# Fewer waits for landed gathers on GpSimd, merge's copies in four parts, and another order of SyncE's waits

## The reference, cut to what matters

```python
# block 0: Gaussian-mixture convolution, K = 3
gauss = exp(sum(-0.5 * (attr - mu)**2 / (1e-14 + sigma**2)))      # per edge, 3 weights
msg   = einsum('eko,ek->eo', (x[src] @ g).reshape(E, 3, 64), gauss)
aggr  = segment_sum(msg, dst) / max(count(dst), 1)
y     = silu(aggr + x @ root_w + bias + x)
# block 1: two SAGE layers on the same edges
nbr   = segment_sum(h[src], dst) / max(count(dst), 1)
h     = h @ W_self + nbr @ W_neigh + b                            # relu between the two
```

## Time and profile before

| | |
|---|---|
| median of 3 runs | 7992.47 us |
| the profiled execution's own time | 8047.77 us |
| its span | 8045.9 us |
| busy: TensorE, VectorE, ScalarE, GpSimd | 64%, 54%, 34%, 42% of the span |
| L512, GpSimd's gathers | 3136 of 1071 ns mean, 3357.8 us busy, 2680.9 us idle before them |
| the long stage, by GpSimd's gathers | from about 61 us to about 6040 us |

### The profile page before, as it was taken

The page is one execution under the profiler, slowest core; times in us unless marked ns, Lnnn a source line. Parts: engine busy times, 40 slices in busy tenths (PEclk is TensorE's granted clock), DMA queues, the critical chain, the costliest instruction groups (busy, mean ns, idle before and its releaser), DMA issues.

```text
span 8045.9 us, 144868 instructions
## 1 busy us (share of the span) xinstructions
PE 5141.5 (64%) x35195; PEld 4042.1 (50%) x35196; DVE 4379.7 (54%) x15088; ACT 2772.2 (34%) x8317; POOL 3360.0 (42%) x3146
## 2 busy tenths in 40 slices
PE   1555555555555555555555555555554699999999
PEld 1223333333444444443334333443443699999999
DVE  5667778766777666655555555555553422222222
ACT  3112333334444444455555555555451100000000
POOL 5013444445666666666666666666650000000000
PEclk5557888877787787777777777777775699999999
DMA  2001111112222222222222222222221399999998
GB/s 68 28 23 56 55 65 65 64 64 68 85 85 85 85 70 86 85 79 75 85 85 76 78 85 85 73 80 85 85 84 42 134 381 382 381 368 385 385 384 346
DMA packets 258352, 1082.32 MB, mean 135 GB/s; under 512 B 140102, under 2 KB 144230, under 8 KB 194406
## 3 DMA queue, kind: packets, MB, share of 16 engines
q1 hardware_dynamic: 142806, 968.66, 31.2%
q0 software_dynamic: 100352, 102.96, 5.6%
q10 hardware_dynamic: 14902, 8.11, 0.5%
HBM read 751.67 MB, written 327.81 MB: 134 GB/s over the span
## 4 chain that ended last, share of the span: by engine, by line
PE 34%; issue 19%; DVE 18%; DVEq 12%; POOL 7%; DMA 4%; ACT 3%; another core or an unknown queue 1%; SPq 1%; ACTq 0%; POOLq 0%
PE pw L965 20%; POOL rE L512 7%; PE pw L795 6%; DVE rE L1264 5%; PE pw L820 3%; DVEq L1297 3%; DVEq L1467 3%; DMA rE<-in_x,idx 2%; DVE rE L1262 2%; DVE rE L1324 2%; PE pw L767 2%; DVE rE L1390 1%; DMA tab<-tab_d 1%; DVE rE L1389 1%; DVEq L1264 1%
## 5 line engine op out<-in xcount | busy, mean ns | idle before, releaser
L512 POOL DMA_INDIRECT rE<-in_x,idx x3136 | 3357.8, 1071 | 2680.9 <-issue 2495.7
L795 PE MATMUL pw<-rE 128*128 128x193 f32 x7824 | 1774.0, 391 | 946.3 <-DVE rE L1324 813.8
L595 ACT CAST rB<-pw 128x792 bf16<-128x792 f32 x1568 | 1252.7, 813 | 3247.8 <-PE pw L820 1081.7
L795 PEld LDWEIGHTS pw<-rE 128*128 128x128 f32 x7824 | 1620.9, 232 | 1163.7 <-DVE rE L1324 983.0
L558 ACT ACTIVATE rE<-rE,cols 128x64 f32<-128x64 f32 x4704 | 1255.0, 344 | 9.3 <-DMA tab<-tab_d 8.2
L820 PE MATMUL pw<-rE 128*128 128x396 f16 x3840 | 822.3, 362 | 669.8 <-DVE rE L1264 471.2
L1264 DVE TENSOR_SCALAR rE<-iperm,gr 128x392 f16<-128x392 f16 x3840 | 1062.3, 317 | 9.7 <-issue 8.8
L820 PEld LDWEIGHTS pw<-rE 128*128 128x128 f16 x3840 | 370.4, 104 | 1060.1 <-DVE rE L1264 547.1
L814 PE MATMUL pw<-rE 128*128 128x396 f16 x1600 | 449.0, 396 | 648.2 <-DVE rE L1390 483.9
L965 PE MATMUL pw<-rB,rA 128*128 128x192 bf16 x9604 | 810.8, 246 | 0.1
L965 PE MATMUL pw<-rE,rA 128*128 128x192 bf16 x9604 | 810.4, 246 | 0.1
(11 more groups left out here) (256 smaller groups left out, 2669.2 us busy)
## 6 DMA issues: line engine op xcount, KB each, us to landing
rA<-count SPq DMA_DIRECT2D x392, 1568.0 KB, 8.4
count<-rB SPq DMA_DIRECT2D x98, 3136.0 KB
rE<-in_x,idx POOLq DMA_INDIRECT x3136
cols<-cols_d SPq DMA_DIRECT2D x98, 64.0 KB
cols_d<-rA SPq DMA_DIRECT2D x3, 1568.0 KB, 5.2
rA<-in_edge_attr ACTq DMA_DIRECT2D x1, 4608.0 KB
out<-gcol ACTq DMA_DIRECT2D x97, 32.0 KB, 6.0
count<-rB SPq DMA_DIRECT2D x8, 224.0 KB, 2.0
```

The lines of the kernel that those rows point to most:

```text
L512: pool.indirect_dma_start(out=gath[:, s, u * CB + b, :], out_offset=None, in_=x, in_offset=bass.IndirectOffsetOnAxis(ap=idx[:, s, u * CB + ...
L595: act.copy(stage[:, s, :, j * 2 * W:(j + 1) * 2 * W].rearrange("p h (w n) -> p w h n", w=2), pu[j % 3][:, :, 0:CW].rearrange("p w (h n) -> ...
L795: ins = pe.matmul(sums[side][:, 0:AW], onehot[:, side, bb, :], wgath[:, side, bb, :], start=(bb == 0), stop=(bb == CB - 1))
```

## The change

Four edits:

1. GpSimd waits for landed gathers (L516) only behind groups 1 and 3 of a tile. Behind groups 0 and 2 it goes on to the waits for the next group's place.
2. In SyncE's pass the wait for the four groups of tile t + 1 and the load of the indices of tile t + 3 move from the pass's start to its end.
3. `merge_ahead(t + 1)` moves from behind unit n = 9 to behind unit n = 4.
4. ScalarE's 32 copies, which stood behind unit 12, are made in four parts of 8, behind units 6, 7, 8 and 9. Only in tile 47, where the copies for tile 48 are made, they stay in one piece behind unit 12.

```diff
             def after(part, t, s, last=False, rows=True):
                 base = PARTS[part][0]
-                if rows:
-                    for u in range(U):
-                        sp.wait_ge(a_g[1 - s][u], (t + base + s) * (8 * CB) + 16 * CB)
-                        sp.sem_inc(s_tick[4], 1)
-                    load_idx(t + (base + 3), 1 - s)
                 sp.wait_ge(a_evac, t * NU + (base * NU + NU + 2))
 ...
                     load_cols(t + (base + 2), s)
+                if rows:
+                    for u in range(U):
+                        sp.wait_ge(a_g[1 - s][u], (t + base + s) * (8 * CB) + 16 * CB)
+                        sp.sem_inc(s_tick[4], 1)
+                    load_idx(t + (base + 3), 1 - s)
```

```diff
-                        pool.wait_ge(a_g[s][u], 16 * CB * (i + 1))
-                        pool.sem_inc(s_tick[1], 1)
+                        if u % 2:
+                            pool.wait_ge(a_g[s][u], 16 * CB * (i + 1))
+                            pool.sem_inc(s_tick[1], 1)
```

```diff
-            def copied(t, s):
-                act.wait_ge(a_mrg, t * 8 + (2 - 8 * TM))
-                act.sem_inc(s_tick[2], 1)
-                act.load(places, tab[0:1, s * TW_:s * TW_ + T_B0])
-                for j in range(JW):
+            def copied(t, s, part=None):
+                if not part:
+                    act.wait_ge(a_mrg, t * 8 + (2 - 8 * TM))
+                    act.sem_inc(s_tick[2], 1)
+                    act.load(places, tab[0:1, s * TW_:s * TW_ + T_B0])
+                for j in range(JW) if part is None else range(8 * part, 8 * part + 8):
...
-                ins.then_inc(a_mrg, 1)
+                if part is None or part == 3:
+                    ins.then_inc(a_mrg, 1)
...
-                        if merged and j == NU - 4:
+                        if merged == "first" and j == NU - 4:
                             copied(i * 2 + (s + 1), 1 - s)
+                        if merged == "parts" and 6 <= j < 10:
+                            copied(i * 2 + (s + 1), 1 - s, j - 6)
```

```diff
-                        if n == NU // 2 + 1 and not last:
+                        if n == 4 and not last:
                             merge_ahead(t + 1)
```

More of the change, by code:

```diff
@@ L573, in copied, with windows @@
                     ins = act.copy(both[:, :, j], gr[:, bass.ds(at, 2)])
-                ins.then_inc(a_mrg, 1)
-            def windows(i, s, last, merged=False):
+                if part is None or part == 3:
+                    ins.then_inc(a_mrg, 1)
+            def windows(i, s, last, merged=None):
                 act.wait_ge(a_st[s], 16 * i + 1)
@@ L611, in _ @@
             windows(TM // 2 - 1, 0, False)
-            windows(TM // 2 - 1, 1, False, True)
+            windows(TM // 2 - 1, 1, False, "first")
             with act.Fori(0, (NT - TM) // 2 - 1, 1) as i:
                 for s in range(2):
-                    windows(i + TM // 2, s, False, True)
-            windows(NT // 2 - 1, 0, False, True)
+                    windows(i + TM // 2, s, False, "parts")
+            windows(NT // 2 - 1, 0, False, "parts")
             windows(NT // 2 - 1, 1, True)
```

## The result

The changed kernel takes 7649.33 us (median of 4 runs, 7645.0 to 7651.4) where the kernel before takes 7993.4 (median of 4, 7985.57 to 8002.84). The ratio is 0.957, 95% interval 0.955 to 0.959: 344 us less. Forecast were 7732 and 260 us less; the time lies in the range, at its fast end. The profiled execution took 7651.4 us, its span is 7649.6.

What follows compares the result with a forecast made beforehand. GpSimd's gather row was taken to bound the kernel, 53.8 us a tile. GpSimd would give 79 + 204 = 283 us, the users 248; 260 was taken, 8048 to 7788 profiled, 7732 as median, range 7640 to 7880.

Steps and rivals of the forecast that it cites:

- GpSimd paces, and two landing waits of four go: GpSimd's gather row sets the tile; two gaps fall from 2.79 to 0.30 us, 5.0 us a tile, to 48.8.
- The price of store against landing: SyncE's store at random phases stretches GpSimd's landing waits by up to 5.7 us; 0.9 us a tile taken.
- R1: Store locks onto GpSimd's landing wait, or VectorE's `tab` wait counts fully: pace 51 to 52.5, 7837 to 7912 us; 22%.
- merge_ahead and the copies: VectorE waits 5 us more for `tab` at unit 4, 3.0 less for copies; users' pace 47.1 to 49.1.
- the stretch before tile 48: Users gain only 18 us over 25 tiles at 51.0; tile 48's gathers start at 3271, 79 us earlier.
- Tiles 0 to 23 stay: The first tiles gain nothing from the change; tiles 6 to 15 stay at 71 us a tile.
- The indices behind the store: Index loads leave later; GpSimd begins up to 7 us later, covered by 16.63 us idle: nothing, at most 7 once.
- The second rule: Denser VectorE doesn't lengthen GpSimd's gathers (1.056 against 1.057 us): nothing; if it did, 0.4 us a tile, 20 in all.
- R3: Faster still: stores miss the landing waits, VectorE's ring hides `tab`; pace 48.8 or less, 7662 us or below; 5%.
- R2: GpSimd's group boundary without landing wait isn't free, about half of 2.79 us stays: pace 51, 7837 us; 7%.
- R4: Sixteen gathers can't be under way, the ninth waits for the queue: GpSimd's tile stays, 7992 us; 3%.
- R5: Slower: full `tab` wait at unit 4 plus a landing wait stretched 5.7 us every tile; 8057 us at 55.5; 6%.

Runs made afterwards that it cites:

- e8_sp_alone: The kernel before with only SyncE's new order (wait for tile t + 1's gathers and index load moved to the pass's end): 8151.49 us, ratio 1.019.
- e13_pool16_behind_store: The kernel before with one landing wait in sixteen gathers, and a tile's first gather waiting for the last issued store to land: 7629.79 us, ratio 0.954.
- e4_pool_and_sp: The kernel before with one landing wait in sixteen gathers and SyncE's new order, merge_ahead and copies as before: 7618.65 us, ratio 0.953.
- e5_wait_once_in_32: The changed kernel with one landing wait in thirty-two gathers, at a tile's end: 7637.35 us, ratio 0.955 to the kernel before.
- e11_pool32_and_sp: The kernel before with SyncE's new order and one landing wait in thirty-two gathers, merge_ahead and copies as before: 7481.29 us, ratio 0.935.
- e7_pool16_tiny_store: The kernel before with one landing wait in sixteen gathers, storing 1/98 of the bytes per tile, most counts behind the last tile: 48.75 us a merged tile.
- e12_copies_in_one_piece: The changed kernel with the 32 copies in one piece as before: 7687.06 us, ratio 0.961 to the kernel before.
- my first four: On one chip: the kernel before unchanged 1.000, with only GpSimd's fewer landing waits 1.058; the changed kernel without those 1.013, with SyncE's old order 1.042.

## Why the prediction was right, and where not

*GpSimd paces, and two landing waits of four go: right.* The gap without a landing wait is 0.30 us in every tile, the low end that I took. The tile was put at 48.8 without collisions and 49.7 with them; 49.1 is measured. The merged tiles give 230 us where I had 204.

*The price of store against landing: the mechanism right, the size by place.* I took 0.9 us a tile at random phases. With two waits the phases are not random: the store never comes earlier than 21.7 us into GpSimd's tile, at 26 us in the median tile and 40.5 at the latest; that is mostly just behind the one landing wait (the second group's gathers end at 20 to 24), and the end gap is 3.34 us instead of 3.2. With four waits the same order costs 57.06 - 53.8 = 3.3 us a tile and the kernel becomes 1.9% slower (e8_sp_alone). So R1 is real, with edit 2 and without edit 1. And edit 2 did not have to be there for the gain: e13_pool16_behind_store has the old order and 0.954, against 0.953 of e4_pool_and_sp.

*merge_ahead and the copies: the sizes near, the sign of the pair right, and its place in the sum wrong.* I gave the wait for `tab` 5 us a tile (3 to 6 as its mark): 172.1 / 49 = 3.5, with single waits of 6. `tab` is used 11.65 us behind the store's issue, 11.6 were reckoned. Of the 3.0 us at the copies 22.7 / 49 = 0.5 is left. The users' pace, forecast at 49.1, is 48.6 where it can be seen alone (e5_wait_once_in_32), and without edits 3 and 4, put at 47.1 at most, it is 46.3 or less (e11_pool32_and_sp). So the two edits slow the users by 2.3 us or more, and cost 33 us even where GpSimd paces. The prediction had the plus of 5 and minus of 3 and did not draw the conclusion that the pair is a loss.

*The step that failed is the stretch before tile 48.* "Before tile 48 the users gain little: 25 tiles from 2088 at 51.0", and so 248 us for the users and tile 48's gathers at 3271 at best. They started at 3180.5. The 51.0 us were read from the earlier trace rows of a profile in which register instructions came late 3.4 times a tile; the users' pace there is 48.8 (e5_wait_once_in_32 and e11_pool32_and_sp, tiles 24 to 47, with GpSimd waiting 5.4 us a tile for them), and 48.9 with SyncE's old order (e13_pool16_behind_store, from the first multiply of tile 24's rows on VectorE, L1307 before, to that of tile 48), so it is not edit 2 that made them faster. With 48.8 in place of 51.0 the prediction's own sum gives, as an estimate, tile 48's gathers at 3220, 130 + 204 = 334 us for GpSimd and 73 + 230 = 303 for the users: 303 instead of 248 decides. The rest of the miss is who paces. The sum let GpSimd keep its lead up to tile 48 and be held only by the place in `gath`. In the changed kernel the lead, from a tile's first gather to its first L1312 (was L1307), falls from 93 us at tile 24 to 40 at tile 48: GpSimd is the slower one there too, at 51.0 us a tile with gathers of 1.077 us.

*"Tiles 0 to 23 stay", "tiles 6 to 15 stay at 71 us": the profiles say no (-80 us; 67.3 us a tile), the experiments say that they probably do.* All eight undisturbed profiles with full stores reach tile 24 between 1956.5 and 1964.6 us, among them the one with SyncE's old order (e13_pool16_behind_store, 1964.6), so the order gives 8 us at most there. The disturbed ones are later: 2036.2 in the profile of before, which as a whole was 55 us too long, and 2056.2 to 2141.1 on the slow chip. How the 344 us divide among the first 48 tiles can't be told closer, as there is no undisturbed profile of the kernel before. e7_pool16_tiny_store reaches tile 24 at 1922.2: the stores themselves cost some 40 us in these tiles, though nothing measurable from 48 on (48.75 against 48.86).

*The indices behind the store: right.* In tiles 5 to 19 GpSimd waits 21 us at a tile's end and the load that comes later is hidden in it.

*The second rule.* I argued from two equal means (1.056 and 1.057) that a denser VectorE doesn't lengthen a gather, and put the rule at nothing. The means hide it. In the merged tiles of e4_pool_and_sp 452 gathers with no VectorE instruction beside them take 0.945 us, and 162 that are mostly beside L1308 (L1307 of the kernel before) take 1.25; in e12_copies_in_one_piece there are again 162 of these and they take 1.42. Of the 0.8 us a tile by which the gathers of e12_copies_in_one_piece are longer, 0.6 is beside L1308 and 0.3 beside the tensor_scalars of L1391. The Trainium skill, "SBUF — State Buffer", section "Who interferes with whom", names VectorE instructions with two inputs in SBUF against a GpSimd operation that reads SBUF. L1308 is a tensor_tensor with two such inputs, GpSimd takes the gathers' indices from SBUF, and the trace agrees in direction. The same section reports a probe in which tensor_tensor did not stall a DMA; that these gathers are longer beside L1308 does not agree with it. So this lengthening is more than half of what edit 3 costs while GpSimd paces (0.8 of 1.35 us a tile); that L1308 causes it is read from what runs at the same time, and no run here took L1308 away.

*The rivals.* R2 (a boundary that isn't free) fell with the 0.30, and R4 as it was priced too. But sixteen gathers are hardly ever under way at once: a gather has landed 1.2 us behind its end (median of e11_pool32_and_sp), when the next one is being made. R5's two conditions never met. The forecast's own band, 200 to 320 us, was missed; the time lies in the range because that reached down to 7640, into R3. The measured gain is R3's, "faster still", 330 us and more, which I gave 5%: too little, since its main obstacle was the users' pace that a disturbed profile had shown too slow.

## What to carry to other kernels

Where one engine's row paces a loop, shorten that row and leave the others' waits alone: edits that removed waits elsewhere cost time here (edit 2 without edit 1, and edits 3 and 4 as a pair), by putting a store or VectorE's work beside what the pacing engine does, and the pair cost more (156 us instead of 33) once GpSimd waited less. After each such step find out who paces now (here: does GpSimd's end gap hold more than a landing?) before the next.

Compare a profile's own time with the median of the runs before reading a pace from it. This one was 0.7% too long, and the pace that decided the forecast was 2.2 us a tile too slow in it. And an experiment that contradicts a sum so plainly deserves one run of the unchanged and of the changed kernel on the same chip: the changed one was missing among my first four, and I built a theory on the difference.

## What was not expected of the hardware

- Chips differ: the medians of the same kernel are 8142 and 8145 us on one and 7993 to 7998 wherever else it was timed. The slow one shows register instructions of up to 1.41 us on ScalarE instead of 0.16 and standstills of three engines at once; from 6600 us on, in the dense stages, none is late there. On it, more gathers in a row made the kernel 5.8% slower, although tiles run at the same gather times (1627.44 / 1568 = 1.038 us).
- A row of 32 indirect gathers without any landing wait runs at 0.30 us between them like a row of 8, and a group's last data land 1.2 us behind its last gather's end (median, e11_pool32_and_sp; 6.0 us at the 95th percentile).
- A 3.2 MB store stretches a landing wait that it meets from 2.9 to 8.6 us, but costs nothing in the merged tiles where no landing wait meets it: 48.75 us a tile with 1/98 of its bytes, 48.86 with all.
- TensorE's granted clock in the merged tiles rose from 0.76 to 0.80 of full speed as the loop got shorter by 9%. Whether that is cause or consequence no run here separates.
